# A 200-column memset on GpSimd behind each of the 782 stores of a scatter

## The reference, cut to what matters

```python
def _scatter_add(tgt, idx, src, axis=0):
    return tgt.at[idx].add(src)
...
x = -0.0002117 + 1 * jax.random.normal(jax.random.fold_in(_gk, 1), (6250, 256), jnp.float32)
src = jax.random.randint(jax.random.fold_in(_gk, 2), (100000,), 0, 6250, jnp.int32)
dst = jnp.minimum((6250 * jax.random.uniform(jax.random.fold_in(_gk, 3), (100000,)) ** 2.0).astype(jnp.int32), 99999)
_o = jnp.argsort(dst, stable=True)
src = src[_o]
dst = dst[_o]
edge_weight = jax.random.uniform(jax.random.fold_in(_gk, 14), (100000,), jnp.float32, 0.0, 0.999998)
```

## Time and profile before

| what | value |
|---|---|
| time, median of 3 runs | 6407.51 us (6405.33 to 6414.07) |
| the profiled execution: its span | 7249.7 us |
| TensorE busy | 5328.2 us, 73% of the span |
| VectorE busy | 3382.5 us, 47% |
| GpSimd busy | 3860.9 us, 53% |
| first scatter, first to last store | 171.9 to 1240.8 us |
| last operation of B0 on VectorE | 2010.4 us |
| second scatter, first to last store | 3478.3 to 4682.2 us |

### The profile page before, as it was taken

How to read it: one execution, slowest core, us unless ns; L and a number is a source line. 1 busy time by engine, 2 the same in 40 slices (tenths; PEclk the granted TensorE clock), 3 DMA queues, 4 the chain that set the end, 5 groups by cost and what they waited for, 6 DMA issues and landing times.

```text
span 7249.7 us, 87859 instructions
## 1 busy us (share of the span) xinstructions
PE 5328.2 (73%) x24977; PEld 4445.0 (61%) x24977; DVE 3382.5 (47%) x9891; ACT 1308.8 (18%) x2962; POOL 3860.9 (53%) x4349
## 2 busy tenths in 40 slices
PE   0111110667659999999899999979999899997794
PEld 0000000556537777777678887868788778876682
DVE  8511100666645555555464464436444554446323
ACT  0000000111101111111142242214111231111240
POOL 0777776000055555555888888830666326654205
PEclk9755555778779999999999999989999999999895
DMA  1000000221133333335310011021333223353223
GB/s 37 9 12 12 12 12 11 73 66 58 59 105 98 96 99 100 98 97 93 49 48 18 14 40 34 20 70 48 91 95 97 76 71 107 108 93 109 89 94 117
DMA packets 319771, 477.56 MB, mean 66 GB/s; under 512 B 99008, under 2 KB 240054, under 8 KB 319470
## 3 DMA queue, kind: packets, MB, share of 16 engines
q0 software_dynamic: 153136, 262.81, 14.8%
q1 hardware_dynamic: 166334, 211.17, 9.5%
HBM read 371.27 MB, written 102.33 MB: 65 GB/s over the span
## 4 chain that ended last, share of the span: by engine, by line
PE 57%; another core or an unknown queue 13%; DVE 11%; issue 11%; DMA 4%; DVEq 2%; ACT 1%; SPq 1%; POOL 1%; ACTq 0%; POOLq 0%
PE bank L2277 13%; PE bank L2288 13%; PE bank L2505 5%; PE bank L2338 5%; PE bank L2487 4%; PE bank L2323 4%; PE bank L2774 3%; PE bank L2630 2%; PE bank L2268 2%; PE bank L2816 1%; DMA sb_work_QT<-scratch_q 1%; DMA sb_rows<-scratch_xn,sb_row_of 1%; DMA sb_work_XC<-in_x 1%; DVE sb_STATE L1391 1%
## 5 line engine op out<-in xcount | busy, mean ns | idle before, releaser
L995 POOL DMA_INDIRECT sb_rows<-scratch_xn,sb_row_of x1760 | 1718.7, 977 | 1553.2 <-PE bank L2323 619.1
L988 POOL DMA_INDIRECT scratch_sorted<-sb_FREE x1564 | 1589.6, 1016 | 546.5 <-issue 379.2
L2288 PE MATMUL bank<-sb_work_FT,sb_W 128*128 128x250 f32 x4400 | 1006.9, 380 | 19.6 <-ACT sb_work_FT L1075 15.1
L2288 PEld LDWEIGHTS bank<-sb_work_FT,sb_W 128*128 128x128 f32 x4400 | 845.3, 193 | 134.6 <-ACT sb_work_FT L1075 22.0
L1075 ACT ACTIVATE sb_HT<-bank,sb_cols 128x250 f32<-128x250 f32 x1333 | 552.8, 467 | 2047.2 <-PE bank L2487 811.6
L2277 PE MATMUL bank<-sb_W,sb_HT 128*125 128x256 f32 x4000 | 894.2, 380 | 1.1 <-ACT sb_HT L1075 1.1
L2277 PEld LDWEIGHTS bank<-sb_W,sb_HT 128*125 128x125 f32 x4000 | 752.7, 188 | 115.4 <-ACT sb_HT L1075 1.9
L2277 PE MATMUL bank<-sb_W,sb_work_FT 128*125 128x256 f32 x1600 | 409.3, 406 | 449.8 <-issue 378.3
L2277 PEld LDWEIGHTS bank<-sb_W,sb_work_FT 128*125 128x125 f32 x1600 | 315.0, 201 | 518.0 <-issue 450.5
L2323 PE MATMUL bank<-sb_rows,sb_work_TM 128*125 128x257 f32 x1760 | 444.8, 392 | 91.2 <-issue 29.7
L1660 DVE TENSOR_TENSOR sb_FREE<-sb_FREE,bank 125x257 f32 x440 | 186.1, 423 | 698.0 <-PE bank L2323 455.1
(11 more groups left out here) (375 smaller groups left out, 7606.2 us busy)
## 6 DMA issues: line engine op xcount, KB each, us to landing
sb_rows<-scratch_xn,sb_row_of POOLq DMA_INDIRECT x1760
scratch_sorted<-sb_FREE POOLq DMA_INDIRECT x1564
scratch_qT<-sb_work_QF SPq DMA_DIRECT2D x100, 250.0 KB
sb_work_QF<-scratch_qT SPq DMA_DIRECT2D x100, 250.0 KB
sb_work_XC<-in_x SPq DMA_DIRECT2D x50, 250.0 KB
sb_work_ZT<-scratch_xn SPq DMA_DIRECT2D x50, 250.0 KB
sb_W<-in_L_mix_W SPq DMA_DIRECT2D x9, 1024.0 KB
sb_work_XC<-scratch_zs SPq DMA_DIRECT2D x28, 256.0 KB, 2.6
```

Of the source, the lines that this page charges most:

```text
L988: nc.gpsimd.indirect_dma_start(out=sorted_d[e], out_offset=bass.IndirectOffsetOnAxis(ap=pos[e][0:n, c:c + 1], axis=0), in_=rec[e][0:n, 2 * ...
L995: nc.gpsimd.indirect_dma_start(out=rows[:, t % RING, 0:D], out_offset=None, in_=table, in_offset=bass.IndirectOffsetOnAxis(ap=row_of[:, t: ...
L2288: ins = nc.tensor.matmul(dst[:, b, :], w[:, k0 + k, 128 * (b0 + b):128 * (b0 + b) + 128], source[:, k, :], start=(n == 0), stop=(n == 2 * ...
```

## The change

Behind each of the 782 stores of the first scatter stands a memset of 200 columns of `rest`, as behind those of the second one of 320 columns. The constant `PACED`, which was 0, goes, and `pause` takes the number of columns. The memsets count on through both scatters.

```diff
-PACED = 0
...
-            def pause(n):
+            def pause(n, columns):
 
                 if n:
                     pool.wait_ge(rested, n)
-                nc.gpsimd.memset(rest[:], 0.0).then_inc(rested, 1)
+                nc.gpsimd.memset(rest[:, 0:columns], 0.0).then_inc(rested, 1)
 
             for c in range(EC):
                 scatter(0, c)
-                if c < PACED:
-                    pause(c)
+                pause(c, 200)
...
             for c in range(EC):
                 scatter(1, c)
-                pause(PACED + c)
+                pause(EC + c, 320)
```

## The result

The changed kernel takes 6503.98 us (median of 4 runs, 6500.5 to 6512.59), the kernel before 6406.42 us (median of 4 runs): a ratio of 1.0148, with an interval of 1.0134 to 1.0163. It is slower by 97.6 us. The forecast was 6500 us.

What follows compares the result with a forecast made beforehand. B0's end and the first scatter's end were taken to meet at the entry to C0, so lengthening the scatter delays everything behind: 1274 - 1180 = +94 us on 6407.5, about 6500 us, range 6395 to 6540.

Steps and rivals of the forecast that it cites:

- both ends of its sum: Entry to C0: 1180 us before the change, 1274 us after it; their difference was the forecast +94 us.
- The 842 us lie ahead of the entry: Profiled span minus timed median, 842.2 us, all placed before the entry to C0, putting the timed entry at 1169 us.
- The crawl is a property of the recorded execution: Stage A0's slow steps beside the first scatter, 843.4 us, come with recording; timed runs hardly have them.
- The entry before at 1180, 1241 at most: C0's entry in timed runs of the kernel before: 1180 us taken, between 1169 and 1241 us.
- rival 2: First scatter ends before B0 even when paced, so the time stays 6407 us; chance 0.10.
- The memset and the spacing: First scatter: a 200-column memset takes 267 ns; stores then start 1.39 to 1.42 us apart.
- The scatter's new end at 1274: Paced first scatter ends at 1274 us, between 1258 and 1282 us, and sets the entry to C0.
- The waits on the store four back held GpSimd 2.4 us: First scatter: waits for earlier stores' landing held GpSimd 2.4 us in all; wider spacing leaves more room.
- The other parts cost nothing of their own: Counter wait and landing waits add nothing; time the memsets give back in A0 and B0 can't be cashed in.
- Pacing frees more: Unpaced stores delay A0 and B0 in timed runs too; entry before at 1314, time falls to 6368 us; chance 0.13.
- The scatter is hidden anyway: Timed stores are fast enough that the paced first scatter ends before B0; time stays 6407 us; chance 0.10.
- The gap doesn't shrink: First scatter keeps 0.30 us issue behind each memset: spacing 1.54 us, end 1376, time 6604 us; chance 0.03.

Runs made afterwards that it cites:

- the disturbed execution: First profiled execution of the unchanged kernel before, in which stage A0 ran slowly beside the first scatter; span 7249.7 us.
- the second recording: The kernel before, unchanged, recorded once more: 6408.06 us, with a span of 6406.2 us.
- the scatter off the path: First scatter cut to 391 of 782 stores, against the kernel before (6281.71 us) and the changed kernel with its 200-column memsets (6296.25 us).

## Why the prediction was right, and where it was not

The forecast of 6500 us is 4 us from the measured 6504, and its sign and its place were right: slower, at the entry to C0, by the last store of the first scatter. But both ends of its sum were 130 to 140 us too early, and the errors took each other away. That the number came out so close is luck: the prediction gave no reason why the two errors should be alike. Step 5 gives one that was found afterwards.

1. *The 842 us lie ahead of the entry.* This step failed. Behind the entry the disturbed execution took 7249.7 - 2011.55 = 5238.2 us, the second recording 5095.6: 142.6 us of the 842 lay behind. The argument was that A0's crawl alone makes 843 us. It does by the count of steps, but the steps' 843 and the entry's shift are two things: the timed entry was no longer B0's end. The mark of the loss behind the entry was in the rows: the 142.6 us that VectorE waited for "remote". In the second recording and in that of after no engine has a wait with that name; that the two sums agree to the tenth is chance, since some 23 us of the loss lie elsewhere: between the entry and the first gather, 31.3 us in the disturbed trace and 8.4 in the second recording, where VectorE's work behind B0 had been done under the wait for the scatter.

2. *The crawl is a property of the recorded execution.* Half of it stands: the timed runs of this kernel didn't have it. But it doesn't come with recording, as the spans of 6406.2 and 6504.5 us show. The Trainium skill's page "NOTIFIC — the notification-queue block", section 7.1, on a block that holds its producers back, had been put behind this step; the runs give it no support, and they don't show what the disturbance was. It stays open.

3. *The entry before at 1180, 1241 at most.* It was 1310.64. B0's end was right (1168 forecast, 1163.8 measured), the scatter's end was not: 1165 forecast from a spacing of 1.27 us, 1309.5 measured at 1.456. The 1.27 came from stores that ran while A0 hardly moved, and no row had stores beside A0 at its own pace; that the spacing "holds at 1.27 us whether the others crawl or not", as rival 2 was answered, was not read from any.

4. *The memset and the spacing.* The memset of 267 ns measured 292 in the mean and 0.28 us undisturbed. The spacing of 1.39 us was 1.41 undisturbed. The sum by spans was rightly left: 228.7 us of memsets cost 104.7. The Trainium skill's rule on starts ("Perfetto Trace Analysis", "Per-instruction lifecycle") agrees with that here: the commonest step from start to start is 1.41 us against 1.26 before, 0.15 us x 781 = 117 us, and 13 us less of waits and longer stores bring it to 104, the shift of the last store.

5. *The scatter's new end at 1274.* It was 1413.8. The mean spacing of the second scatter, 1.540 us with 320 columns, was carried over with 117 ns less, but the first scatter has more beside it: 1.589 us with 200 columns, 1.640 with 320. This is the same cause as in step 3, landing waits and longer stores, mostly beside A0 and B0: 153 us over 781 steps of 1.26 before, 140 us over 781 steps of 1.41 after. As it lengthens the first scatter of both kernels nearly alike, the difference of +94 us stood while both its ends fell.

6. *The waits on the store four back held GpSimd 2.4 us.* This failed as a term of the timed runs: 108.7 us before, 72.1 after. It had been read off the trace in which A0 crawled, and the claim that these waits cost nothing hid the one change that gains.

7. *The other parts cost nothing of their own.* Not quite: B0 ends 15.7 us later (1178.78 for 1163.10), and 16.8 us with the scatter off the path. It was covered, as the scatter ends last.

The rivals. *Pacing frees more*: its premise came true almost to the number (145 us behind the entry, an entry at 1314), and its outcome didn't, since the paced scatter's end wasn't 1274 but grew with the unpaced one's. *The scatter is hidden anyway* falls: it ended 146 us behind B0. *The gap doesn't shrink* falls: 0.17 us, as in the earlier trace rows.

Of the marks named ahead, the memsets, A0 at 27 to 28 us a step, the span of 6504.5 and the releaser of the load came as written. The spacing of 1.39 to 1.42 us came only where hardly anything ran beside the scatter. The load stood 130 us behind the stretch named for it, and TensorE was idle for 234 us ahead of it instead of 100. These two said that the ends were wrong while the difference was right.

## What to carry to other kernels

Where a profiled execution is much longer than the timed ones, record the kernel once more before building a sum on it: the disturbed trace misled here not only on the stages that crawled, but on the stores beside them. Where the end of a long train of small stores releases the next stage, price a delay by the steps from start to start, and read the waits for landings beside the real load: allowing more stores in flight took 70 us off the path, and a pause between them added 105.

## What the runs showed of the hardware

**A store's landing beside other transfers.** The median over both scatters is 2.4 us, in the page's list of DMA issues (engine, operation, count, us to landing) of after:

```profile
scratch_sorted<-sb_FREE POOLq DMA_INDIRECT x1564, 2.4
```

Beside B0 the chain of waits of after holds landings of over 8 us (start, us, what):

```profile
1107.84 8.04 DMA scratch_sorted<-sb_FREE
...
1148.25 8.42 DMA scratch_sorted<-sb_FREE
```

In the first scatter alone the longest landing is 9.3 us here, and 9.0 with eight in flight. Four in flight at 1.26 us cover 5 us; eight cover 10, and no wait was left. What of the load beside them delays the landings wasn't taken apart.

**A store on GpSimd beside VectorE's work.** With eight in flight, where no store waits, the 139 stores ahead of B0's end beside which VectorE ran nothing took 0.97 us at most. All 19 that took over 2 us stand beside a few operations of VectorE: 8 beside L1391 to L1395, of the sort that runs beside A0, and 11 beside L1631 and L1635, the end of a step of B0, as here:

```profile
754.41 1.29 DVE L1631 TENSOR_TENSOR sb_work_TM<-sb_work_TM,sb_rowA 125x512 f32<-125x512 f32 x2
754.57 3.17 POOL L988 DMA_INDIRECT scratch_sorted<-sb_FREE  x1 [0.30 <-issue]
755.61 1.29 DVE L1635 TENSOR_TENSOR sb_work_KT<-sb_work_KT,sb_work_TM 125x512 f32<-125x512 f32 x2
```

So the longer stores go with VectorE's operations, and the landing waits are another matter. That VectorE holds the stores up is argued from where they stand; no run took these operations away.

**Memsets on GpSimd and VectorE.** One operation of VectorE in A0 takes longer beside the longer memsets: 418 ns before, 459 with 200 columns, 566 with 320, but 412 with 64 (lines of 262 to 1164 us of the first three, in this order):

```profile
L1330 DVE TENSOR_SCALAR sb_work_ZT<-sb_work_XC,sb_MV,sb_RY 125x256 f32<-125x256 f32 x50 | 17.8, 418 | 2.5 <-DVE sb_RY L1298 2.4
```

```profile
L1328 DVE TENSOR_SCALAR sb_work_ZT<-sb_work_XC,sb_MV,sb_RY 125x256 f32<-125x256 f32 x50 | 20.0, 459 | 2.5 <-DVE sb_RY L1296 2.4
```

```profile
L1328 DVE TENSOR_SCALAR sb_work_ZT<-sb_work_XC,sb_MV,sb_RY 125x256 f32<-125x256 f32 x50 | 25.4, 566 | 2.5 <-DVE sb_RY L1296 2.4
```

The same operation on an input from TensorE's output banks (L1330, then L1328, `bank`) hardly changes: 536, 538 and 536 ns. B0's last operation starts at 1163.10, 1178.78 and 1201.87 in these three, and at 1163.33 with 64 columns. All of VectorE's work from 172 us to B0's end is 674.3, 681.0 and 722.9 us: 6.7 us more for a delay of 15.7, and 48.6 more for 38.8. So the slower operations go with the delay, but with 200 columns they don't add up to it, and its cause isn't shown.
